# A pairwise-product tower on one core: half-length sums on ScalarE, ordered by a counter, and second copies issued by SyncE

## The reference

```
e = stack([tbl_f[ids[:, f]] for f in range(40)], axis=1)       # 512 x 40 x 64
viW = einsum('bpd,pde->bpe', e[:, i_idx], W)                   # W: 780 x 64 x 64
z = einsum('bpe,bpe->bp', viW, e[:, j_idx])                    # 512 x 780
h = relu(concat([z, dense_ctx], 1) @ W_top1 + b_top1)          # 796 -> 512
h = relu(h @ W_top2 + b_top2)                                  # 512 -> 256
y = h @ W_top3                                                 # 256 -> 1
```

## Time and profile before

| | |
|---|---|
| runs | 354.84 us median of 3 |
| profiled execution, its own time | 354.51 us |
| its span, first to last instruction | 352.3 us |
| mean granted TensorE clock | 0.976 |
| TensorE matmul busy | 316.6 us (90%) |
| VectorE busy | 250.2 us (71%) |
| ScalarE busy | 219.1 us (62%), without the DMAs it issues |
| GpSimd busy | 233.1 us (66%) |

### The profile page before, as it was taken

The page is one execution under the profiler, slowest core; times in us unless marked ns, Lnnn a source line. Parts: engine busy times, 40 slices in busy tenths (PEclk is TensorE's granted clock), DMA queues, the critical chain, the costliest instruction groups (busy, mean ns, idle before and its releaser), DMA issues.

```text
span 352.3 us, 5566 instructions
## 1 busy us (share of the span) xinstructions
PE 316.6 (90%) x1472; PEld 112.1 (32%) x1472; DVE 250.2 (71%) x252; ACT 219.1 (62%) x1696; POOL 233.1 (66%) x194
## 2 busy tenths in 40 slices
PE   0799865999959899999889999999999969999997
PEld 0133423333223333332223333333233323333442
DVE  2375782888728788989759999999999959940000
ACT  1001200467979779779969898897999979600032
POOL 6777777777777767753883899799894953920000
PEclk9999996999989999999989999999999989999999
DMA  6733452333322327632122411423311200000000
GB/s 170 229 105 93 111 146 56 87 97 107 86 58 89 86 79 262 199 95 69 47 75 60 110 45 57 117 64 97 83 41 55 60 0 1 2 0 2 0 0 0
DMA packets 17865, 27.66 MB, mean 79 GB/s; under 512 B 4901, under 2 KB 5029, under 8 KB 17834
## 3 DMA queue, kind: packets, MB, share of 16 engines
q1 hardware_dynamic: 9770, 17.86, 16.9%
q0 software_dynamic: 4608, 4.73, 6.1%
q10 hardware_dynamic: 3456, 4.72, 4.7%
HBM read 22.57 MB, written 0.00 MB: 64 GB/s over the span
## 4 chain that ended last, share of the span: by engine, by line
PE 44%; ACT 25%; POOL 11%; DVE 7%; issue 6%; ACTq 4%; DMA 1%; DVEq 0%
ACT batched L371 24%; PE ps_t L538 18%; PE ps_t L521 8%; PE ps_z L560 7%; POOL rows L319 6%; PE ps_t L586 5%; DVE prod L446 5%; POOL wide_rows L319 5%; ACTq L355 4%; PE ps_t L621 2%; PE ps_e L586 2%; DVE batched L460 2%; PE ps_e L500 1%; ACT E L348 1%; DMA rows<-in_tbl,ids_sb 1%
## 5 line engine op out<-in xcount | busy, mean ns | idle before, releaser
L371 ACT ACTIVATE batched<-batched 128x64 f32<-128x64 f32 x832 | 198.8, 242 | 40.0 <-DVE batched L460 16.6
L446 DVE TENSOR_TENSOR prod<-ps_t,E 128x1024 f32<-128x1024 f32 x148 | 170.9, 1216 | 29.5 <-PE ps_t L538 27.5
L371 ACT ACTIVATION_READ_ACCUMULATOR batched<-batched 128x1 f32 x832 | 156.5, 188 | 0.0
L538 PE MATMUL ps_t<-E,w_sb 64*128 64x512 f32 x592 | 147.4, 621 | 5.5 <-ACT E L348 3.4
L319 POOL DMA_INDIRECT rows<-in_tbl,ids_sb x128 | 121.3, 948 | 38.1 <-issue 37.8
L326 POOL TENSOR_TENSOR prod<-prod 128x1024 f32<-128x1024 f32 x40 | 93.6, 2371 | 32.8 <-DVE prod L446 32.6
L538 PEld LDWEIGHTS ps_t<-E,w_sb 64*128 64x128 f32 x592 | 51.6, 187 | 89.7 <-issue 55.7
L460 DVE TENSOR_TENSOR batched<-ps_t,wide_rows 128x1024 f32<-128x1024 f32 x52 | 60.4, 1218 | 19.4 <-PE ps_t L521 19.2
L521 PE MATMUL ps_t<-w_sb,E 64*128 64x512 f32 x208 | 51.5, 637 | 8.2 <-issue 8.2
L560 PE MATMUL ps_z<-prod,quads 128*32 128x512 f32 x352 | 52.6, 611 | 0.0
L348 ACT ACTIVATE E<-ps_e 128x512 f32<-128x512 f32 x18 | 10.5, 583 | 41.1 <-PE ps_e L489 22.7
(11 more groups left out here) (41 smaller groups left out, 60.8 us busy)
## 6 DMA issues: line engine op xcount, KB each, us to landing
w_sb<-in_w_units SPq DMA_DIRECT2D x50, 256.0 KB, 2.7
E<-E ACTq DMA_DIRECT2D x72, 64.0 KB, 2.1
rows<-in_tbl,ids_sb POOLq DMA_INDIRECT x128
w_sb<-in_w SPq DMA_DIRECT2D x7, 256.0 KB
prod<-in_ids_by_field SPq DMA_DIRECT2D x2, 512.0 KB, 9.1
prod<-in_tbl SPq DMA_DIRECT2D x3, 312.5 KB
w_sb<-in_w SPq DMA_DIRECT2D x1, 512.0 KB
wide_rows<-in_tbl,ids_sb POOLq DMA_INDIRECT x16, 4.3
```

The lines of the kernel that those rows point to most:

```text
L371: last = act.activation(products, products, ACT.Copy, accum_out=zt[:, b, at:at + 1])
L446: dve.tensor_tensor(prod[:, n % P_RING, s, :, :], ps_t[:, step % STEPS, :, :], multiplier, ALU.mult).then_inc(product_ready, 1)
L538: last = pe.matmul(ps_t[:, step % STEPS, j, :], w_sb[at:at + DIM, m % W_RING, col:col + P], E[at:at + DIM, slot_of(pairs_of(n)[s][j]), :], ...
```

## The change

1. ScalarE's sums come in halves of a quarter: 8 activations instead of 16, so there are 104 of them. Semaphore counts of `batched_summed` are doubled everywhere.
2. A counter decides how many halves stand in ScalarE's list at each place: a group adds 5, a batched unit 10, a half takes 4, a copy of an arrival takes 2.
3. The four DMAs of an arrival to `E4` are issued by SyncE from F6 on (48 of 72, since F18 and F19 have none); F0 to F5 stay with ScalarE.
4. The first two batched units use couples 13 and 11 instead of 14 and 12, most batched units stand one unit later, and F6 and F7 stand directly ahead of the group that needs them. So g6, g7 and g8 now stand between F5 and F6, and r20 comes ahead of B4 where it came behind it.

The numbers of groups, steps, batched units, gathers and adds stay as they are.

```diff
-BATCHED = (14, 12, 10, 9, 8, 7, 6, 5, 4, 3, 2, 1, 0)
-BATCHED_AT = (4, 6, 10, 13, 17, 20, 24, 27, 31, 34, 38, 41, 45)
+BATCHED = (13, 11, 10, 9, 8, 7, 6, 5, 4, 3, 2, 1, 0)
+BATCHED_AT = (3, 7, 11, 14, 18, 21, 24, 28, 31, 35, 38, 42, 45)
...
 def ahead(u):
-    return 1 if u < 12 else 2
+    return 0 if u in (6, 7) else 1 if u < 12 else 2
...
+PACE = {"group": 5, "batched": 10}
+SUM_COST, COPY_COST = 4, 2
+
+BY_SCALAR = 6
...
+        def place_fields(eng, u):
+
+            k = KP - 1 - u
+            if k < 2:
+                return
+            eng.wait_ge(e_copied, place(u) + 1)
+            for f in range(2):
+                for h in range(2):
+                    to, of = (2 * (k % 2) + f) * HALF, f * DIM + h * HALF
+                    eng.dma_start(E4[to:to + HALF, k // 2 - 1, h, :], E[of:of + HALF, slot_of(k), :]).then_inc(
+                        e4_placed[u], 16)
...
             for kind, at in order():
-                if kind == "fields" and at == PARAMS_AT:
-                    load_params()
+                if kind == "fields":
+                    if at == PARAMS_AT:
+                        load_params()
+                    if at >= BY_SCALAR:
+                        place_fields(sp, at)
...
-            def sum_batched(j, b):
+            def sum_batched(j, b, i):
 
                 act.wait_ge(product_ready, FIRST_STEP["batched", j] + b + 1)
-                for i in range(2):
-                    for f in range(WIDE):
-                        at = (2 * j + i) * WIDE + f
-                        products = batched[:, (BT * j + b) % B_RING, i, f, :]
-                        last = act.activation(products, products, ACT.Copy, accum_out=zt[:, b, at:at + 1])
+                for f in range(WIDE):
+                    at = (2 * j + i) * WIDE + f
+                    products = batched[:, (BT * j + b) % B_RING, i, f, :]
+                    last = act.activation(products, products, ACT.Copy, accum_out=zt[:, b, at:at + 1])
                 last.then_inc(batched_summed, 1)
...
-            left = []
+            left, time = [], 0
             for kind, at in order():
                 if kind == "fields" and at >= FIRST:
                     copy_fields(at)
+                    time -= COPY_COST
                 elif kind == "rows":
                     copy_rows(at)
-                elif kind == "batched":
-                    left += [(at, b) for b in range(BT)]
-                elif kind == "group" and left:
-                    sum_batched(*left.pop(0))
+                elif kind in PACE:
+                    if kind == "batched":
+                        left += [(at, b, i) for b in range(BT) for i in range(2)]
+                    time += PACE[kind]
+                    while left and time >= SUM_COST:
+                        sum_batched(*left.pop(0))
+                        time -= SUM_COST
+                    if not left:
+                        time = min(time, 0)
```

More of the change, by code:

```diff
@@ L339, in copy_fields @@
             def copy_fields(u):
-                k = KP - 1 - u
                 if u < LOOKED_UP:
@@ L347, in copy_fields @@
                     act.wait_ge(e4_placed[u - E_RING], 64)
[L348 to L356, removed]
+                act.activation(E[:, u % E_RING, :], e_bank[u], ACT.Copy).then_inc(e_copied, 1)
+                if u < BY_SCALAR:
+                    place_fields(act, u)
             def copy_rows(u):
@@ L379, in _ @@
                     copy_fields(at)
+                    time -= COPY_COST
                 elif kind == "rows":
                     copy_rows(at)
-                elif kind == "batched":
-                    left += [(at, b) for b in range(BT)]
-                elif kind == "group" and left:
-                    sum_batched(*left.pop(0))
-            assert len(left) <= (B_REST // (2 * WIDE)) * BT
+                elif kind in PACE:
[7 more added lines that the diff above has]
+                        time = min(time, 0)
+            while left and left[0][0] < P // (2 * WIDE):
+                sum_batched(*left.pop(0))
             act.wait_ge(zt_turned, 1)
             act.activation(z[:, CHUNKS, :], turn_bank[0], ACT.Copy).then_inc(zt_copied, 1)
-            for j, b in left:
-                sum_batched(j, b)
+            for half in left:
+                sum_batched(*half)
             act.wait_ge(zt_turned, 2)
@@ L457, in multiply_batched @@
                     if at >= B_RING:
-                        dve.wait_ge(batched_summed, at - B_RING + 1)
+                        dve.wait_ge(batched_summed, 2 * (at - B_RING + 1))
                     dve.wait_ge(step_done, step + 1)
@@ L597, in _ @@
             pe.wait_ge(e_copied, KP)
-            pe.wait_ge(batched_summed, BT * (P // (2 * WIDE)))
+            pe.wait_ge(batched_summed, 2 * BT * (P // (2 * WIDE)))
             turn_zt(0)
@@ L612, in _ @@
                 sum_h1(m, range(CHUNKS - 1, CHUNKS + 1))
-            pe.wait_ge(batched_summed, BT * NB)
+            pe.wait_ge(batched_summed, 2 * BT * NB)
             turn_zt(1)
```

## The result

The changed kernel takes 341.14 us (median of 4 runs, 340.66 to 341.38), beside 355.68 for the kernel before in the same comparison: a ratio of 0.9587, 95% interval 0.9545 to 0.9629. The prediction was 342 us, from 334 to 350. The profiled execution has a span of 339.6 us (339.1 was worked out) and a mean granted clock of 0.99. Engines do the same work as before within a microsecond or so, except TensorE, whose busy time falls from 316.6 to 311.5 us as fewer records are slow.

The account below looks back on a forecast made before the run. TensorE was taken to bound the kernel, standing 19.1 us for F6's gather and late ScalarE copies. Gains of 13.2 us took the span from 352.3 to 339.1; plus 2.2 and 0.3, about 342 us, range 334 to 350.

Parts of the forecast that it names:

- Groups 6 to 8 ahead of F6: Up to g27: work fills F6's 6.95 us wait, F7's copy holds TensorE 2.3 us, g27 ends at 133 us.
- GpSimd's second add takes part back: At r20: the add ends at 139.5, TensorE stands 6 us, hiding changes before it; the gain there is 10.3 us.
- From r20 to g73: The stretch behind r20's start takes 157.5 us, so g73 ends at 297.1 instead of 310.3, 13.2 us earlier.
- ScalarE's near tie: From F15 to F19 ScalarE needs 85 us, TensorE 86.7, with 3.63 us of room at each copy.
- without gaps: Sign to look for: ScalarE works from F15 to F19 with no idle time, its last sum near 297 us.
- The DMAs to E4: Twelve arrivals from F6 on: 2.44 us of issuing each leaves ScalarE, up to 2.4 on SyncE costs nothing; no separate gain.
- r20 not binding: At r20: TensorE does not wait for the adds, r20 starts at 133, total 334 us; chance 0.10.
- The second: In the second half: ScalarE stays late, F14's and F19's waits remain, 8.9 us of gain goes, 351 us; chance 0.14.
- The chain: At arrivals F13 to F19: transposes, halves, copy and next groups wait in turn, 4.5 us lost each, 373 us; chance 0.06.
- no change: Whole kernel: copies come in time but something else sets the same pace, 353 to 356 us; chance 0.08.
- ScalarE's share hides at most some 27 us of stalls: Kernel before: ScalarE's 25% of the chain of waits stands for at most some 27 us of TensorE stalls.

Follow-up runs that it names:

- e1: The changed kernel with GATHER_LEAD 13 instead of 14, so F14's gather stands behind both adds of r20: 334.48 us.
- e7: The changed kernel with GATHER_LEAD 20 instead of 14, so the gathers of F14 and F15 stand ahead of r20's adds: 351.06 us.
- e8: The changed kernel without the adds of g20 and g21, r20 summing 16 records instead of 8, gathers behind F14's 4.8 us earlier: 335.44 us.
- e2: The changed kernel with part 3 undone, so ScalarE issues the DMAs to E4 of all arrivals: 345.77 us.
- e4: The changed kernel with parts 1 and 2 undone, so ScalarE sums whole quarters, one after each group: 340.83 us.
- e3: The kernel before with part 3 alone, in the old order with the old list of whole quarters: 340.38 us.
- e9: The changed kernel with part 4 undone, so halves, counter and SyncE's issues in the old order: 338.48 us.
- e10: The kernel before with parts 3 and 4 and GATHER_LEAD 13 instead of 14, sums in whole quarters: 332.61 us.
- e6: The kernel before with parts 1 and 2 alone, old order, ScalarE issuing all DMAs to E4: 351.61 us.
- e5: The kernel before with part 4 alone, whole quarters one after each group, ScalarE issuing all DMAs to E4: 348.87 us.

## Why the prediction was right, point by point

- *Groups 6 to 8 ahead of F6.* Right: F6's transposes start without a wait, at 58.46 where 57.3 was worked out; the 1.80 for F5's gather, which was not foreseen, lies ahead of them. F7's copy held TensorE by 2.61 us where 2.3 was worked out; g27 ended at 133.9, not 133. r20's wait hid this.
- *GpSimd's second add takes part back.* Right, and the term with the most to lose: r20 at 140.01 for 139.6, held by 6.03 us. e1, e7 and e8 move this wait, each with other shifts of the later gathers, and the end of the kernel moves with it each time. That up to 6 us ahead of it don't count is shown by e2, where some 8 us are lost ahead of r20 and r20 starts 2.0 later. e4 shows less of it, as F8's and F9's gathers took back most of what F7 gained.
- *From r20 to g73.* 157.5 was worked out; the last couple ends at 297.5, so 157.5 was measured. That it is exact is in part luck: the sum of pieces has two slips, nine batched blocks of 8.11 are 73.0, not 73.8, and there are seven arrivals behind r20, so transposes take 4.1, not 2.4. Put right, it gives 156.0 instead of 155, which is the 156 that was taken between two estimates. The slow records behind the wait cost 0.9 at r20 and, against B4 in e1, 0.9 there: 1.8 for the 1.5 taken.
- *ScalarE's near tie.* Right: F15's transposes to F19's take 86.8 us (86.7 worked out) and ScalarE waits in between, by 2.22 for F15 and 0.72 for F18, so it is a little faster, and the sign "without gaps" did not hold. The last sum ends at 295.1 instead of 297.
- *The DMAs to E4.* On SyncE an arrival costs 2.41, the upper end that was taken, and no engine waits for them to land. But "no term of its own" undersold it. The sum was made over the places where time is lost, and did not say which part of the change removes each loss; there the experiments say more. Part 3 is worth 15 us alone (e3), parts 1 and 2 nothing that these runs can tell beside it (the change against e4, e9 against e3, e1 against e10: 0.3 more, 1.9 less and 1.9 more, intervals overlapping or just touching), part 4 nothing or less as long as r20 waits (the change against e9) and 4 to 8 us once it doesn't (e1 against e9, e10 against e3; both pairs also differ in the place of the gathers).
- *The rivals.* The first, r20 not binding, gives 334 by the same sum; e1 built it: 334.48. The second is what e2 shows at 345.77, by way of the ring of sums rather than of copies. The chain and no change did not come.
- *A bound that was not worked out.* That ScalarE's share hides at most some 27 us of stalls has no sum behind it; the waits of 19.1 us and the slow records listed beside them come to about 25.

## What to carry to other kernels

Before a queue's order is tuned, look at what stands in it that needn't: four DMA issues of 0.6 us an arrival, in the list of an engine near its tie, cost 4.0% of the time, of 6.5% that the fastest kernel here won, and a finer order of that engine's sums won next to nothing. When a stall is removed, follow each other engine's list to the point where something else arrives last: one gather of 9.9 us between two adds took back what the new order had won, could be worked out from rows of before, and a constant moved by one gave it back (6.7 us by the medians of e1 and the change).

## What the runs showed of the hardware that was not expected

Whether TensorE is slow behind a wait of some 2 to 3 us differs between like places. After F7's wait of 2.61 in the changed kernel the couple took 3.70; after 2.75 at the same place in e8 it took 5.40:

```profile
70.75 5.40 PE L558 MATMUL ps_t<-E,w_sb 64*128 64x512 f32 x16 [2.75 <-issue]
```

At this place e1 (2.51) goes with the change, e2 (2.75) and e7 (2.68) with e8. But the length of the wait alone doesn't decide it: in e6 eight records took 3.37 behind a wait of 1.69, in e5 1.99 behind one of 2.83 (their rows are above). Stretches with busy time of PE, PEld, DVE, ACT, POOL, then the granted clock, DMA share and GB/s; first the changed kernel (the couple behind F7's wait, r20's wait, r20 with B4), then e8 (the couple behind F7's wait), last e6 (behind the wait of 1.69):

```profile
70.60:74.20 3.60, 3.59 (x16) 1.56 (x16) 2.35 (x3) 3.60 (x32) 2.84 (x3) 1.00 0.36 100
...
134.00:140.00 6.00, 0.00 (x0) 0.02 (x1) 2.17 (x2) 4.86 (x41) 5.18 (x4) 0.75 0.30 86
140.00:146.40 6.40, 6.39 (x24) 2.01 (x24) 2.34 (x3) 0.00 (x0) 4.85 (x6) 0.70 0.10 21
```

```profile
70.75:76.10 5.35, 5.35 (x20) 2.39 (x20) 3.15 (x3) 5.35 (x47) 3.83 (x6) 0.68 0.31 74
```

```profile
198.20:201.70 3.50, 3.41 (x12) 1.14 (x16) 3.33 (x4) 3.50 (x31) 3.48 (x3) 0.58 0.08 21
```

The clock was at 2.4 GHz throughout behind F7's wait in the changed kernel, and at means of 0.68 and 0.58 of it, so partly at 1.2 GHz, in e8 and e6. For such a wait anything from nothing to 1.7 us of slow matmuls has to be reckoned with; behind the waits of 6 us and more all that were looked at had them.
